# Attention block of a metaformer on one core: first step written out stage by stage, a second weight buffer, two batch splits in later steps

## The reference

```python
x = x + _L0_conv_ref(_ln_c(x), gamma, beta, qkv_w, qkv_b, proj_w, proj_b)
t = _to_tokens(x)                    # (4, 1024, 256)
t = t + _L0_ffn_ref(_ln_t(t))
x = _from_tokens(t, x)
# _L0_conv_ref, on xf of shape (b, 256, 1024):
qkv = conv1d_same(group_norm(xf, gamma, beta), qkv_w, qkv_b)  # 16 taps, 768 out
qkv = qkv.reshape(b * 4, -1, t)      # 4 heads of 64 channels
h = qkv_attention(qkv)               # softmax(q k^T / 8) v
h = conv1d_same(h.reshape(b, -1, t), proj_w, proj_b)          # 5 taps
return xf + h
# _L0_ffn_ref: hot = x_bd > 0.5; three argmaxes over 16 columns give lo, hi and a
# shift; (lo + 16*hi) is shifted left or right by it, masked by columns 0, 39 and
# 40, and 2 * one_hot of the two nibbles is added to columns 64:80 and 72:88
```

## Time and profile before

| | |
|---|---|
| median of 3 runs | 1192.69 us (1190.08 to 1196.02) |
| profiled execution | 1190.26 us, span 1188.5 us |
| mean granted TensorE clock | 0.942 |
| busy of the span | PE 1016.5 us (86%), DVE 862.2 (73%), ACT 575.1 (48%), POOL 231.3 (19%) |
| DMA | 120.44 MB, mean 101 GB/s |
| chain that ended last | PE 45%, DVE 31%, issue 9%, DMA 6%, ACT 5%, POOL 3% |

### The profile page before, as it was taken

One profiled execution on the slowest core, in us unless ns is written; L12 is line 12 of the kernel. 1 busy time (PEld: TensorE's weight loads), 2 busy tenths in 40 slices (PEclk: granted clock), 3 DMA queues, 4 the chain that ended last, 5 costly groups with the idle time before them and its releaser, 6 DMA issues.

```text
span 1188.5 us, 17778 instructions
## 1 busy us (share of the span) xinstructions
PE 1016.5 (86%) x6760; PEld 670.0 (56%) x6760; DVE 862.2 (73%) x1655; ACT 575.1 (48%) x794; POOL 231.3 (19%) x164
## 2 busy tenths in 40 slices
PE   2737395999999999997989899999999998988854
PEld 1425262666566655664655466656666666756644
DVE  7985976767576578786868566667658675988867
ACT  3443343545445445645547355544435455555522
POOL 2541724100000113112121100000010003223221
PEclk9859697999999999998989899999999999999987
DMA  4240105375275435651654157426533763434412
GB/s 147 80 180 25 45 28 214 74 159 93 50 164 112 80 71 127 145 85 36 195 120 77 36 122 146 89 54 156 95 71 72 191 127 87 107 60 100 107 54 71
DMA packets 279775, 120.44 MB, mean 101 GB/s; under 512 B 267665, under 2 KB 270097, under 8 KB 276753
## 3 DMA queue, kind: packets, MB, share of 16 engines
q1 hardware_dynamic: 279696, 119.37, 43.5%
HBM read 37.43 MB, written 14.81 MB: 44 GB/s over the span
## 4 chain that ended last, share of the span: by engine, by line
PE 45%; DVE 31%; issue 9%; DMA 6%; ACT 5%; POOL 3%; SPq 1%; DVEq 0%; ACTq 0%; POOLq 0%
PE cP L838 11%; PE cM L838 10%; PE cQ L838 8%; PE psV L905 8%; DVE arena L1218 4%; DVE smx L1228 4%; DMA arena<-arena 3%; PE psS L865 3%; PE psT L865 3%; DMA H<-w_qkv 2%; DVE W L1012 2%; DVE W L1005 2%; POOL wsum L466 2%; ACT arena L709 1%; DVE arena L1026 1%
## 5 line engine op out<-in xcount | busy, mean ns | idle before, releaser
L838 PE MATMUL cM<-U,W 128*128 128x256 f16 (+1 forms) x1536 | 230.3, 307 | 47.8 <-ACT m_sb L693 17.8
L838 PE MATMUL cP<-U,W 128*128 128x256 f16 (+1 forms) x1536 | 227.5, 305 | 17.0 <-DVE yqk L1066 11.9
L709 ACT ACTIVATE arena<-arena,smx 128x1024 f16<-128x1024 f32 x128 | 146.8, 1147 | 173.2 <-DVE smx L1261 170.9
L838 PE MATMUL cQ<-U,W 128*128 128x256 f16 (+1 forms) x1536 | 220.6, 300 | 0.0
L838 PEld LDWEIGHTS cM<-U,W 128*128 128x128 f16 x1536 | 152.4, 99 | 120.4 <-ACT m_sb L693 18.1
L838 PEld LDWEIGHTS cP<-U,W 128*128 128x128 f16 x1536 | 151.6, 99 | 84.9 <-DVE yqk L1066 12.2
L838 PEld LDWEIGHTS cQ<-U,W 128*128 128x128 f16 x1536 | 149.2, 97 | 65.1 <-issue 1.6
L1218 DVE SCALAR_TENSOR_TENSOR arena<-arena,smx 128x1024 f16<-128x1024 f32 x128 | 167.6, 1309 | 20.0 <-ACT arena L709 19.9
L905 PE MATMUL psV<-arena 128*128 128x512 f16 x512 | 124.0, 398 | 37.4 <-DMA arena<-arena 37.4
L1270 DVE SCALAR_TENSOR_TENSOR arena<-psV,arena 64x512 f32<-64x512 f32 x32 | 22.0, 689 | 152.0 <-ACT arena L716 151.9
L687 ACT ACTIVATE arena<-psS,smx,esc 128x1024 f32<-128x1024 f32 x64 | 76.9, 1202 | 75.1 <-DVE smx L1229 75.1
(11 more groups left out here) (196 smaller groups left out, 1235.6 us busy)
## 6 DMA issues: line engine op xcount, KB each, us to landing
U<-kept_u SPq DMA_DIRECT2D x6, 2077.0 KB, 9.9
H<-w_qkv SPq DMA_DIRECT2D x12, 1024.0 KB, 7.6
kept_u<-U SPq DMA_DIRECT2D x2, 2077.0 KB, 10.3
kept_u<-arena SPq DMA_DIRECT2D x2, 2077.0 KB, 6.9
arena<-x_tok SPq DMA_DIRECT2D x8, 512.0 KB, 9.0
W<-x_tok SPq DMA_DIRECT2D x4, 1024.0 KB, 6.1
out_tok<-W SPq DMA_DIRECT2D x3, 1024.0 KB, 4.3
kept_h<-arena SPq DMA_DIRECT2D x4, 514.0 KB, 4.5
```

What stands on the lines that cost most here:

```text
L709: a(phl[:, i % 3, 0, :], prob[:, i % 2, :], ACT.Copy, scale=smx[:, i % 2, 4:5]) \
L838: last = mm(out, W[:, j, wl, c, wat + tap, :], U[:, slot, ul, c, at:at + width], start=(c == 0 and tap == 0 and wl + ul == 0), stop=(c == ...
```

## The change

**The first step** is written as a list of stages on every engine (`first_step()`), and no table serves it. Inputs come in the order 0, 1, 3, 2 (`BATCH_AT`; q counts the place in it). On ScalarE the stages of tile 1 stand behind m_sb, and the ones of the two tiles are set alternately. Batches at q = 2 and 3 are normalized and transposed there, but not split.

**Second buffer.** `wst_b`, in the arena's end where `aside` was, takes tile 1; its load waits for nothing. `load_w` issues four pieces of 512 KB. Tile 2 waits for tile 0's lo parts.

**Splits in later steps.** The two late batches are split in slots 3, 5 and 7 of steps 1 and 2, straight into the ring. One's even/odd form stays in DRAM meanwhile (`keep_eo`, `load_eo`, 1040 KB each way). `load_u` then is needed from step 4 on only, in four pieces.

**Weight scale.** ScalarE squares each tile and accumulates (`squares`), VectorE adds the two halves (`wadd`), and the root is taken with the exponent. `wtop` stands a slot behind `wadd`.

**Attention.** The two small scalings L1229 and L1261 become ScalarE activations. The K copies become one DMA of 256 KB a head (`copy_k`), behind turn(k, 4) and turn(k, 14). `scale_y`, `qk_hi` and `qk_lo` are a slot later, `heads` stands in slots 6, 10, 14 and the next step's 0, and loops over steps are written out.

The core of the diff, cut:

```diff
-        aside = arena[:, edge[-1] - CT * UW:edge[-1]].bitcast(F16).rearrange("p (l c w) -> p l c w", l=2, c=CT)
+        WST = CT * 2 * PH_TAPS * P
+        wst_b = arena[:, edge[-1] - WST:edge[-1]].rearrange("p (c s k o) -> p c s k o", c=CT, s=2, k=PH_TAPS)
         wsum = sb("wsum", [P, 2, QTAPS, P], F32)
-        H1 = sb("H1", [P, 2, NB, 2, HW], F16)
-        wst = H1[:, :, :, :, :].rearrange("p a b r w -> p (a b r w)")[:, 0:8192].bitcast(F32) \
-            .rearrange("p (c s k o) -> p c s k o", c=CT, s=2, k=PH_TAPS)
+        staging = sb("staging", [P, 2 * EO], F32)
+        H1 = staging[:, 0:NB * HR // 2].bitcast(F16).rearrange("p (l b r w) -> p l b r w", l=2, b=NB, r=2)
+        wst_a = staging[:, 0:WST].rearrange("p (c s k o) -> p c s k o", c=CT, s=2, k=PH_TAPS)
+        eo_b = staging[:, 0:EO].rearrange("p (c r w) -> p c r w", c=CT, r=2)
+        diff_b = staging[:, EO:2 * EO].rearrange("p (d c w) -> p d c w", d=2, c=CT)
+        sub_b = staging[:, 0:EO].rearrange("p (d c s w) -> p d c s w", d=2, c=CT, s=2)
...
+        BATCH_AT = (0, 1, 3, 2)
+
         def u_home(b):
 
-            return (U[:, 1], U[:, 0], aside, aside)[b]
+            return U[:, (b + 1) % 2]
...
-        WSTAGES = ("wmax0", "wmax1", "wscale", "wsum0", "wsum1", "wsum2", "w00", "w01", "wsum3", "w10", "w11")
-
-        def tile_weights(m, slots):
-
-            return [(slot, (kind, m)) for slot, kind in zip(slots, WSTAGES)]
+        WSTAGES = ("wmax", "wadd", "wtop", "wscale", "wsum0", "wsum1", "wsum2", "w00", "w01", "wsum3", "w10", "w11")
+
+        def tile_weights(m, *slots):
+
+            return [(slot, (kind, m)) for slot, kind in zip(slots, WSTAGES) if slot is not None]
...
         EXTRA = {
-            0: table(batch_input(1, 0, 4, 4, 7, 7, 7, 10), tile_weights(1, (1, 1, 2, 2, 2, 2, 2, 2, 2, 2, 2)),
-                     batch_input(2, 6, 10, 10, 13, 13, 13, 14), tile_weights(2, (8, 8, 9, 9, 9, 9, 9, 9, 9, 9, 9)),
-                     batch_input(3, 13, 16, 15, 17, 17, 17, 17), [(4, ("wtop", 1)), (10, ("wtop", 2)), (17, ("ring", 0))]),
-            3: table(tile_weights(3, (1, 3, 4, 4, 5, 6, 8, 8, 9, 10, 10)), tile_weights(4, (12, 14, 15, 15, 16, 17, 17)),
-                     [(4, ("wtop", 3)), (15, ("wtop", 4))]),
...
+            1: table(batch_split(2, 3, 5, 7), [(1, ("ring", 0))]),
+            2: table(batch_split(3, 3, 5, 7)),
+            3: table(tile_weights(3, 0, 1, 2, 2, 3, 4, 5, 5, 6, 6, 7, 8),
+                     tile_weights(4, 13, 14, 15, 15, 15, 16, 16, 17, 17)),
+            4: table(tile_weights(4, no, no, no, no, no, no, no, no, no, 0, 1, 1),
+                     tile_weights(5, 6, 7, 8, 8, 9, 10, 11, 12, 12, 13, 14, 14), [(16, ("pads", 0))]),
+            STEPS - 1: {8: [("pwmax", 0)], 11: [("pwtop", 0)], 12: [("pwscale", 0)], 13: [("pw", 0)], 14: [("pw", 1)],
                         15: [("base", 0, 0), ("base", 0, 2)], 16: [("base", 0, 4), ("base", 0, 6)]},
...
+            def load_x(q):
+                if q >= 2:
...
-            def load_w(m):
-                if m >= 1:
...
+            def load_w(m, parts=range(2 * CT)):
+                if m >= 2:
+                    sp.wait_ge(S["wlo_done"], PARTS * (1 if m == 2 else m))
+                for q in parts:
+                    c, s = q // 2, q % 2
+                    sp.dma_start(wst(m)[:, c, s].rearrange("p k o -> p (k o)"),
+                                 w_qkv[m, c][:, s * PH_TAPS * P:(s + 1) * PH_TAPS * P]).then_inc(S[f"ws_b{c}" if m == 1 else f"ws_in{c}"], 16)
...
+            def keep_eo():
+
+                sp.wait_ge(S["eo_done"], 4 * 3)
+                sp.dma_start(kept_eo, eo.rearrange("p c r w -> p (c r w)")).then_inc(S["eo_kept"], 16)
+
+            def load_eo():
+
+                sp.wait_ge(S["eo_kept"], 16)
+                sp.wait_ge(S["ulo_done"], SPLITS * 3)
+                sp.dma_start(eo_b.rearrange("p c r w -> p (c r w)"), kept_eo).then_inc(S["eo_in"], 16)
+
+            def copy_k(k, hd):
+
+                sp.wait_ge(S["qk_lo"], 2 * (2 * k + hd + 1))
+                sp.dma_start(stack[0:D, hd, 1:3, :].rearrange("p k t -> p (k t)"),
+                             stack[D:P, hd, 1:3, :].rearrange("p k t -> p (k t)")).then_inc(S["qk_done"], 16)
...
-            sp.wait_ge(S["u_out3"], 16)
+            keep_eo()
+            copy_k(0, 0)
             for k in range(STEPS):
                 for u in range(UNITS):
                     turn(k, u)
                     if u == 1 and 1 <= k <= NB:
                         keep_h(k - 1)
-                    if u == 4 and k < STEPS - 2:
-                        load_u(k + 2)
+                    if u == 4:
+                        copy_k(k, 1)
+                    if k == 0 and u == 9:
...
+                        load_w(5, [2 * u - 2, 2 * u - 1])
+                    if u == 14 and k < STEPS - 1:
+                        copy_k(k + 1, 0)
...
+            def squares(m, c):
+                wait(act, "wam_done", m)
+                weights_in(act, m, c)
+                if m < 3:
+                    junk = W[:, m, 0, c, 0:2 * PH_TAPS]
+                else:
+                    junk = wsum[:, :, :, :].rearrange("p h k o -> p (h k o)").bitcast(F16).rearrange("p (a o) -> p a o", o=P)
+                    act.wait_ge(S["wlo_done"], PARTS * m)
+                    act.wait_ge(S["c_m"], 2 * m + c)
+                a(junk, wst(m)[:, c].rearrange("p s k o -> p (s k) o"), ACT.Square,
+                  accum_out=am[:, 4 + c:5 + c]).then_inc(S["c_m"], 1)
...
+            def first_step():
+
...
+                fine_high(0, 0)
+                extra("w00", 0)
+                extra("w01", 0)
+                squares(1, 0)
+                fine_high(0, 1)
+                main_copy(0, 0, 0)
+                extra("wsum3", 0)
+                fine_high(0, 2)
+                common_copy(0, 0, 0, 0)
+                extra("w10", 0)
+                extra("w11", 0)
+                fine_high(0, 3)
+                squares(1, 1)
+                common_copy(0, 0, 0, 1)
+                extra("wsum0", 1)
...
+                        act.wait_ge(S["mx_done"], 16 * k + u + 1)
+                        a(smx[:, u % 2, 1:2], smx[:, u % 2, 0:1], ACT.Copy, scale=esc[:, hd, 1:2]).then_inc(S["nb_done"], 1)
...
+                    if unit:
+                        act.wait_ge(S["rc_done"], 16 * k + i + 1)
+                        a(smx[:, i % 2, 4:5], smx[:, i % 2, 3:4], ACT.Copy, scale=2.0 ** PROB_BITS).then_inc(S["pn_done"], 1)
                         act.wait_ge(S["pn_done"], 16 * k + i + 1)
...
-                    v.tensor_tensor(am[:, 0:1], am[:, 4:5], am[:, 5:6], ALU.max).then_inc(S["wam_done"], 1)
+                    v.tensor_tensor(am[:, 0:1], am[:, 4:5], am[:, 5:6], ALU.add).then_inc(S["wam_done"], 1)
...
+                dve.wait_ge(S["qk_hi"], 2 * runs + part + 1)
                 if part == 0:
...
-                if part == 2:
-                    ch.wait()
-                    ch.step(v.tensor_copy(stack[0:D, hd, 1, :], stack[D:P, hd, 1, :]))
-                    v.tensor_copy(stack[0:D, hd, 2, :], stack[D:P, hd, 2, :]).then_inc(S["qk_done"], 1)
...
                         dve.wait_ge(S["e_done"], 16 * k + i + 1)
-                        ch.step(v.reciprocal(smx[:, i % 2, 3:4], smx[:, i % 2, 2:3]))
...
+                    if conv and i in (8, 14):
+                        scale_y(3 * n + i // 6 - 1, i // 6 - 1, n)
+                    if attn and i in (3, 4):
+                        qk_lo(i - 3, 1, 2 * k + 1)
+                    if conv and i in (15, 16):
+                        qk_lo(i - 15, 0, 2 * n)
+                    if k >= 1 and i == 0:
+                        heads(k - 1, 3)
```

801 lines of the change are left out of this document (483 added, 318 removed).

## The result

The changed kernel takes 1205.43 us (median of 4 runs, 1203.67 to 1206.36). The kernel before, beside it, took 1190.08, 1192.69 and 1196.02 us; a fourth execution of it took 3784.50 us and is left out. The ratio is 1.0103, 95% interval 1.0068 to 1.0138. It is **slower by 1%**, a small difference that the interval tells from none; the forecast was 1148, with 1122 to 1174 as the range.

What follows compares the result with a forecast made beforehand. TensorE bounds middle steps (near 109.4 us); time above that lies in the first, second and two splitting steps and last stage. -39 + 4 - 2 - 6 + 7 - 8 = -44 from 1192.7 gives 1148 us, range 1122 to 1174.

Steps and rivals of the forecast that it cites:

- first step with step 1: First step and the one after it: 270 us together where they were 309.3, a change of -39.
- step 2: Middle step that takes over batch 3's and parts of batch 2's splitting: +4 us, bounds 0 and +12.
- steps 3 and 4: The two steps that split batches 2 and 3 before (127.7 and 125.6 us): -2 and -6 us.
- steps 5 to 7: Later steps, lengthened at their end by the K copy's place in the DMA order: +7 us together.
- last stage: Final stage, 186.1 us before: K copies and scalings leave VectorE, -8 us, bounds -14 and 0.
- L915(0): Start of batch 0's transposes opening the first attention: at 148 us, not 187.2; sign 140 to 155, wrong after 160.
- QK(0): First attention's QK: starts near 155.5 us, when the K rows land; 6 to 9 us behind the first transposes.
- "-2" for step 3: Weight tile spread over slots 0 to 8, input split gone, VectorE waits for the scale: -2 us, bounds -15 and +4.
- "-6" for step 4: The 5.81 us wait for the weight maximum goes: -6 us, bounds -14 and 0.
- +2.3 a step: Step's end: K copy ahead of turn(15), transpose lands 2 to 4 us later, PV waits about 4.3 instead of 1.95.
- a steady step over 114 us: Middle steps: a length above this was listed as a sign that the prediction is wrong.
- Slower: Rival, chance .04: copies and transposes on one queue exclude each other, 8.2 us a step's end, 5 at slot 4; about 1220.

Runs made afterwards that it cites:

- e8: From e5: in the first step tile 1's sums and parts again stand ahead of tile 0's bank reads; 1184.03 us.
- e11: From e6: tile 1's load waits for tile 0's lo parts, as with a single staging buffer, and its squares stand later; 1161.63 us.
- e5: The mix: changed kernel with K copies on VectorE except the last, and extra stages at their old places in the slot in steps 3 and 4; 1162.61 us.
- e2: Changed kernel with all K copies on VectorE again, behind the second qk_lo, and no DMA; 1187.41 us.
- e9: Changed kernel with one edit on SyncE: the K copy for the next step's head 0 is issued behind turn 15, not ahead; 1181.79 us.
- e6: From e5: heads (the read of PV's result) at their old slots 5, 9, 13 and 17; 1154.64 us.
- e10: From e6: scale_y, qk_hi, qk_lo and the spread of y's maximum at their old places; 1165.82 us.
- e12: Changed kernel with turn 15 before K copy, old stage places in steps 3 and 4, old heads slots, last stage's scale_y, qk_hi, qk_lo at old places; 1151.46 us.
- e3: Changed kernel with the two small scalings of each unit on VectorE again; 1204.03 us.
- e7: From e5: the two small scalings of each unit on VectorE again; 1162.32 us.

## Why the prediction was wrong

Forecast and measured change of the span lie 58.3 us apart (-44 and +14.3). By term: first step with step 1 6.2, step 2 3.5, steps 3 and 4 31.9, steps 5 to 7 7.2, last stage 9.5.

- **The first step: right.** L915(0) forecast at 148, measured 150.6; QK(0) 155.5, measured 156.45. e8 and e11 give the two parts: 20.8 for the order, 7.4 for the buffer, out of 36.6. The rest (squares instead of maxima, the splits moved out) was not run apart. The K copy behind the two large stores landed 9.5 us after its issue, where a K copy's median is 3.6. The Trainium skill ("DMA: Bandwidth & Descriptors", "Queues, rings and completion order") says that a semaphore increment lands only after every earlier write of the same DMA engine. On the engines that both use, the copy's end should then not show before the writes of the store ahead. The one case here agrees: keep_eo landed at 155.28, the copy at 156.41.
- **The step that failed: "-2" for step 3 and "-6" for step 4.** Measured +11.7 and +12.2. The prediction priced the waits that would go and gave the place of the stages no price. The 5.81 us for the maximum in step 4 did go. But it took the *slots* of the table as the stages' places, and the change had also moved them from the start or middle to the end *within* a slot, on three engines, and so closed the cycle of ScalarE and VectorE. That VectorE is busy for 86.8 us of 139.3 says nothing against such a cycle. e5 against e2 gives 9.5 and 10.9 us for the two steps, and the K copy's order 2.7 and 2.4 (e9). Nor did -2 and -6 come without these: in e5 the steps are 127.0 and 125.5, level with 127.6 and 125.7 before. Other waits stand where the old ones went, in e5's step 3 4.98 us before cP (449.37) and 4.61 for ap (503.62).
- **The term that was mis-sized: "+2.3 a step" for the K copy.** The mechanism was named and found in its place (SyncE, turn 15 behind a copy behind qk_lo), 3.7 us of wait against "about 4.3". The price is 3.5 to 5.1 us a step (e9), since matmuls behind the wait run slower (5.12 for 3.61 us). The prediction put a clock's recovery into the first step and the "slower" rival and forgot it here. Its sum has the wait for steps 5 to 7 and, as 3 us, for step 1; steps 2 to 4 have it "in their terms" without a number. e9 shows 1.7 to 3.2 in steps 1 to 4. All in all it is 21.6 us of span. The prediction's own sign of being wrong, a steady step over 114 us, came with it (115.0 in step 5).
- **Steps 1 and 2.** Forecast 122 (from 148 to 270), measured 125.9; forecast +4, measured +7.5. In step 2, e2 gives 3.3 to the K copy and e6 4.8 to heads (against the mix), a move that the prediction's bounds have as one that "pays". Without both, step 2 is 111.1, so the splits that +4 was meant for cost 1.9.
- **The last stage: "-8", measured +1.5.** The DMA copies did bring 7.4 (e2). What it left out is that other edits cost as much: scale_y and qk a slot later 4.4 in e10 (less in e12), heads perhaps 1 to 2, the rest not placed. From the exclusive port the prediction had the next two-input operation wait as long as the copy did. The Trainium skill ("SBUF — State Buffer", "SBUF: two separate sides") has the loser blocked until the other's whole instruction has run, which is a different time, and the rows agree with it. The next operation with two inputs in SBUF, a low part, starts at 1058.97, 1.98 us before GpSimd's L549 ends (1060.95), and takes 3.06 us instead of 1.28, so 1.8 us passed on and no more (L549 is GpSimd's second pass of the layer norm):

```profile
1058.97 3.06 DVE L1428 SCALAR_TENSOR_TENSOR arena<-arena,smx 128x1024 f16<-128x1024 f32 x1
```

```profile
1055.56 5.39 POOL L549 TENSOR_TENSOR W<-W 128x2048 f32<-128x2048 f32 x1
```

- **The rivals.** "Slower" was the right side, for one of its reasons: a turn held behind a K copy. It was priced as a conflict of DMAs (8.2 us and 5 at slot 4). e9 leaves all copies in place and its steps 5 and 6 are 109.9 and 109.6, so the conflict shows only in the 0.7 us that a transpose behind a copy takes longer; the rest of the loss is a place in a written order of instructions. Its sum is also off: +92 less 55 gives some 1230, not 1220.

What stays open: the rest of the last stage's loss, GpSimd's share in steps 3 and 4, and why the old place of qk_lo costs steps 1, 2, 4 and 7 what it does.

## What to carry to other kernels

Read where in its slot a stage stands, on each engine, before and after, and follow one slot round all engines: two engines that hand to each other twice a slot can make a cycle whose length no busy share shows (6.76 us here, with TensorE needing 6.08). A DMA that waits for a late result holds every later one of the engine that issues them; issue first what TensorE waits for (one line, 23.6 us here). Price a wait of TensorE with the slow matmuls behind it.

## What the runs showed of the hardware

- Matmuls 128x512 behind a wait of 3.68 us: sixteen take 5.12 us; behind 1.11 or 1.95 us, 3.61. The wait alone doesn't decide it: sixteen take 3.61 us behind 3.45 too (e3, 893.18), and 5.30 behind 2.02 (the kernel before, 997.31).
- Two VectorE copies 64x1024 float16 in the last stage took 4.62 us each (1034.30 and 1038.96) beside two GpSimd operations, and 4.62 + 0.42 in e2, where GpSimd's operation ended shortly before the second (1036.16).
- A 256 KB copy inside SBUF as a DMA lands in 3.6 us (median of 16, with transposes in flight), where the store of that size took 2.6. A DMA transpose issued right behind such a copy lands 4.98 us after its issue (median of 10), the others 4.32 (118).
- ScalarE's square with accumulation over 128x2048 took 1.89 + 0.19 us, VectorE's maximum over the same 2.28.
- A scaling of 128x1 takes 0.29 us as an activation and 0.21 on VectorE, and which it is made no measurable difference (e7, 0.3 us).
